# Decoder layer on one core: the low part of the mixing's gelu output is computed on GpSimd instead of VectorE

## The reference, cut to what matters

```
attn = (1 - LAMBDA_INIT) * rms(attn, g2)          # per head
attn = rms(attn, g3) + attn                        # "w" of a unit, 256 tokens x 256
h    = gelu(attn @ W1.T)                           # exact gelu
out  = h @ W2.T + attn
x    = x + out                                     # x1 of the unit
...
x = x + cross_attention(layernorm(x), ctx, ctx)    # second block
x = x + moe_ffn(layernorm(x))                      # third block, 8 experts with adapters
```

## Time and profile before

| | |
|---|---|
| median of 3 runs | 699.44 us (698.05 to 700.78) |
| profiled execution | 699.32 us, span of its rows 697.6 us |
| PE busy | 630.2 us, 90% |
| DVE busy | 505.7 us, 72% |
| ACT busy | 367.7 us, 53% |
| POOL busy | 265.1 us, 38% |
| chain that ended last | PE 76%, issue 7%, DVE 6%, DMA 3%, ACT 3%, POOL 2% |

### The profile page before, as it was taken

How to read it: one execution, slowest core, us unless ns; L and a number is a source line. 1 busy time by engine, 2 the same in 40 slices (tenths; PEclk the granted TensorE clock), 3 DMA queues, 4 the chain that set the end, 5 groups by cost and what they waited for, 6 DMA issues and landing times.

```text
span 697.6 us, 21651 instructions
## 1 busy us (share of the span) xinstructions
PE 630.2 (90%) x8338; PEld 591.6 (85%) x8338; DVE 505.7 (72%) x1242; ACT 367.7 (53%) x825; POOL 265.1 (38%) x361
## 2 busy tenths in 40 slices
PE   3789699799878787878999999999999999999997
PEld 3678577587667687767999999999999999999997
DVE  5586288687556988546887877788778877886672
ACT  3545457576673676533655455545554555455432
POOL 1212121221130554233455545554555455534322
PEclk9899999999988999996999999999999999999999
DMA  8684848567683476420001101110111011100000
GB/s 266 125 108 80 120 70 122 92 103 112 98 173 104 138 188 192 150 84 23 24 2 39 39 2 39 38 38 0 38 38 38 0 38 38 38 0 16 16 16 31
DMA packets 84140, 50.13 MB, mean 72 GB/s; under 512 B 31320, under 2 KB 83808, under 8 KB 84064
## 3 DMA queue, kind: packets, MB, share of 16 engines
q1 hardware_dynamic: 84064, 49.07, 31.9%
HBM read 23.88 MB, written 12.58 MB: 52 GB/s over the span
## 4 chain that ended last, share of the span: by engine, by line
PE 76%; issue 7%; DVE 6%; DMA 3%; ACT 3%; SPq 2%; POOL 2%; POOLq 0%; DVEq 0%; ACTq 0%
PE banks L698 58%; PE banks L824 5%; PE banks L753 3%; PE banks L842 3%; PE banks L860 2%; PE banks L983 2%; DMA m_w<-attn_scratch 2%; DMA attn_scratch<-h_wn 1%; POOL f_hT_lo L2138 1%; PE banks L767 1%; SPq L537 1%; DMA n_v<-in_L_attn_Wv_dram 1%; PE banks L722 1%; DVE wqkvT_lo L1542 1%; ACT h_t L1404 1%
## 5 line engine op out<-in xcount | busy, mean ns | idle before, releaser
L2138 POOL TENSOR_TENSOR f_hT_lo<-f_hs,f_hT_hi 128x512 fp32r<-128x512 f32 x64 | 87.3, 1365 | 102.8 <-ACT f_hT_hi L1377 99.2
L1841 DVE SCALAR_TENSOR_TENSOR f_hs<-banks,nbic,f_h 128x256 f32<-128x256 f32 x128 | 54.6, 479 | 40.6 <-PE banks L698 40.6
L698 PE MATMUL banks<-woT_hi,f_hT_lo 128*128 128x256 f32 x256 | 74.8, 292 | 0.2 <-POOL f_hT_lo L2138 0.2
L698 PE MATMUL banks<-f_adT_hi,lbT_lo 128*128 128x256 f32 x256 | 73.5, 287 | 0.0
L698 PE MATMUL banks<-f_xT_hi,wiT_hi 128*128 128x256 f32 x256 | 72.6, 284 | 0.0
L698 PE MATMUL banks<-f_xT_hi,wiT_lo 128*128 128x256 f32 x256 | 72.5, 283 | 0.0
L698 PE MATMUL banks<-woT_hi,f_hT_hi 128*128 128x256 f32 x256 | 72.4, 283 | 0.0
L698 PE MATMUL banks<-f_adT_lo,lbT_hi 128*128 128x256 f32 x256 | 72.4, 283 | 0.0
L698 PE MATMUL banks<-woT_lo,f_hT_hi 128*128 128x256 f32 x256 | 72.3, 283 | 0.0
L698 PE MATMUL banks<-f_xT_lo,wiT_hi 128*128 128x256 f32 x256 | 72.3, 282 | 0.0
L698 PE MATMUL banks<-f_adT_hi,lbT_hi 128*128 128x256 f32 x256 | 72.2, 282 | 0.0
(11 more groups left out here) (265 smaller groups left out, 2008.2 us busy)
## 6 DMA issues: line engine op xcount, KB each, us to landing
h_qk<-p_qk SPq DMA_DIRECT2D x64, 128.0 KB, 5.1
xin<-in_x_dram SPq DMA_DIRECT2D x16, 256.0 KB, 5.5
h_v<-p_v SPq DMA_DIRECT2D x128, 32.0 KB
attn_scratch<-h_wn SPq DMA_DIRECT2D x16, 256.0 KB, 4.6
m_w<-attn_scratch SPq DMA_DIRECT2D x16, 256.0 KB, 2.8
m_x<-in_x_dram SPq DMA_DIRECT2D x16, 256.0 KB, 3.4
x_scratch<-m_y SPq DMA_DIRECT2D x16, 256.0 KB, 2.2
c_x<-x_scratch SPq DMA_DIRECT2D x16, 256.0 KB, 2.8
```

The source lines that it names most:

```text
L698: ins = pe.matmul(acc, left(a), right(b), start=first and n == 0, stop=last and n == 2, skip_group_check=skip)
L1841: ins = dve.scalar_tensor_tensor(out=f_hs[:, j % 2, c * T:(c + 1) * T], in0=bank[HB[j]][:, c * T:(c + 1) * T], scalar=nbic[:, f:f + 1], in ...
L2138: pool.tensor_tensor(lo, f_hs[:, j % 2], hi.bitcast(F32), ALU.subtract).then_inc(f_hlo, 1)
```

## The change

The 16 splits leave DVE's order and are emitted on POOL. What is computed, its operands and its semaphores are the same. On POOL each split n stands behind the x-add of unit n+1 (behind the head step `head_rthird` too, for unit 5, and behind the last piece of `p_final` for unit 0); the splits 14 and 15 come after the last x-add. The orders of PE, ACT and SP are the same as before. The diff, cut in the middle of DVE's order:

```
@@ -1651,11 +1651,6 @@
             def m_low(u):
                 low(u, m_hi, flat(m_aT[u.slot][0][:, :, :]), flat(m_aT[u.slot][1][:, :, :]), bank[TURNED][:, :], m_lo)
 
-            def m_gsplit(u):
-                hi, lo = (flat(m_hT[u.slot][p][:, :, :]) for p in range(2))
-                dve.wait_ge(m_ghi, nth(u, 1, 1))
-                dve.tensor_tensor(lo, m_g[:, :], hi.bitcast(F32), ALU.subtract).then_inc(m_glo, 1)
-
             def m_residual(u):
                 dve.wait_ge(m_o, nth(u, 1, 1))
                 dve.wait_ge(m_xad, nth(u, 1, 1))
@@ -1946,17 +1941,14 @@
             go(4, head_normal, head_gain)
             go(0, m_low)
             go(1, m_low)
-            go(0, m_gsplit)
             go(6, head_masked(1, 0), head_masked(1, 1))
             go(2, m_low)
             go(4, head_added)
-            go(1, m_gsplit)
             go(7, head_masked(0, 0), head_masked(0, 1))
             clear_gate()
             go(0, m_residual)
             go(5, head_sums, head_newton)
             go(3, m_low)
-            go(2, m_gsplit)
             go(5, head_normal)
             go(1, m_residual)
             go(5, head_gain)
...
@@ -2018,11 +2000,10 @@
             go(14, m_low)
             go(12, m_residual)
             low_parts(LAST + 3, LAST + 4)
-            go(13, m_gsplit)
             go(15, m_low)
             go(13, m_residual)
-            go(14, m_gsplit, m_residual)
-            go(15, m_gsplit, m_residual)
+            go(14, m_residual)
+            go(15, m_residual)
 
 
 
@@ -2073,6 +2054,11 @@
                     pool.tensor_scalar(p_qk[:, u.slot, c], p_exp[:, c % 2], -1.0, headfac[:, 0:1] if c < KD else 1.0,
                                        ALU.add, ALU.mult).then_inc(p_fin, 1)
                 return emit
+
+            def m_gsplit(u):
+                hi, lo = (flat(m_hT[u.slot][p][:, :, :]) for p in range(2))
+                pool.wait_ge(m_ghi, nth(u, 1, 1))
+                pool.tensor_tensor(lo, m_g[:, :], hi.bitcast(F32), ALU.subtract).then_inc(m_glo, 1)
 
             def m_with_x(u):
                 if u.index == 0:
@@ -2162,29 +2148,45 @@
             go(0, m_with_x)
             go(1, m_with_x)
             go(7, p_final(3))
+            go(0, m_gsplit)
             go(4, head_rthird)
             go(2, m_with_x)
+            go(1, m_gsplit)
             go(3, m_with_x)
+            go(2, m_gsplit)
             go(0, c_rstds)
             go(5, head_rthird)
             go(0, c_constant)
             go(4, m_with_x)
+            go(3, m_gsplit)
             go(0, c_natural, c_with_bias)
             go(5, m_with_x)
+            go(4, m_gsplit)
             go(6, m_with_x, head_rthird)
+            go(5, m_gsplit)
             go(1, c_rstds)
             go(7, m_with_x)
+            go(6, m_gsplit)
             go(1, c_constant)
             go(8, m_with_x)
+            go(7, m_gsplit)
             go(1, c_with_bias)
             go(9, m_with_x)
+            go(8, m_gsplit)
             go(7, head_rthird)
             go(10, m_with_x)
+            go(9, m_gsplit)
             go(11, m_with_x)
+            go(10, m_gsplit)
             go(12, m_with_x)
+            go(11, m_gsplit)
             go(13, m_with_x)
+            go(12, m_gsplit)
             go(14, m_with_x)
+            go(13, m_gsplit)
             go(15, m_with_x)
+            go(14, m_gsplit)
+            go(15, m_gsplit)
 
 
 
```

More of the change, by code:

```diff
@@ L1652, in m_low @@
                 low(u, m_hi, flat(m_aT[u.slot][0][:, :, :]), flat(m_aT[u.slot][1][:, :, :]), bank[TURNED][:, :], m_lo)
[L1654 to L1657, removed]
             def m_residual(u):
@@ L1998, in _ @@
             go(1, c_clow)
-            go(9, m_gsplit)
             go(11, m_low)
```

12 lines of the change are left out of this document (removed).

## The result

The change made the kernel slower: 711.36 us median of 4 runs (707.60 to 713.77) against 699.02 us of the kernel before (698.05 to 700.78), ratio 1.0156 with a 95% interval of 1.0115 to 1.0196. Measured again beside the experiments, on another chip, it was 709.84 against 700.26 us, ratio 1.0135 (1.0093 to 1.0177). The forecast was 702.6 us, at most 707.0: the direction was the one that it leaned to, the size was three to four times too small. The profiled execution took 711.32 us, its span is 709.6 us.

The account below looks back on a forecast made before the run. The mixing was taken as bound by a chain of handovers, no engine being full, and the last stage by PE. Pass-by-pass terms summed to +3.2 us on 699.32, giving a 702.6 us median; range 699.6 to 707.0.

Parts of the forecast that it names:

- The cost of the operation: On POOL: a split takes 1.30 us, an x-add 1.28 once the split has left DVE.
- The new ready time: In the mixing: split ready 2.75 us after the residual add, 2.15 later than before.
- Pass 4 to 5, +2.1: Between residual adds 4 and 5: 6.45 us instead of 4.36, with the head step's root ahead of split 5 on POOL.
- in the range, not in the sum: Splits 6 to 8 meeting DVE's head steps: slowing of DVE and POOL counted only in the range 700.5 to 706.2 us.
- units 6 and 7, +0.6: Gelu 7 waits for split 6, and c_rr precedes x-add 8: +0.6 us, between 0 and one c_rr.
- pass 7 to 8, +0.8: Between residual adds 7 and 8: a pass as short as 4 to 5, lengthened by 0.8 us.
- I take only what the short passes need: Mixing, eleven passes: the average pass of 5.41 us exceeds the 5.2 minimum, so the 23.7 us upper bound is not charged.
- Up to unit 3 cost 0, relief -0.7: Units up to 3: splits ready long before PE needs them; DVE's relief brings m_aT_lo earlier, -0.7 us taken.
- The gelu of unit 11, +0.3: Passes 9 to 12: the gelu of unit 11 waits for split 10, +0.3 us.
- The last stage passes the shift on: From 312 us on PE is busy 377 of 386 us, so the mixing's 3.2 us shift passes on.
- 1 and 2: DVE's relief decides, 240 to 310 us: 694.1 us (chance 0.05); other slack swallows it: 699.5 to 700.4 us (chance 0.22).
- Rival 3: PE's clock and contention in the mixing: three more slow matmul groups, +3.9 us, 706.5 us; chance 0.15.

Follow-up runs that it names:

- the late splits ahead of the x-adds: Kernel before with splits 5 to 15 on POOL, each ahead of x-add n+1, splits 0 to 4 on DVE: 703.24 us, ratio 1.0033.
- early splits alone: Kernel before with only splits 0 to 4 on POOL, splits 5 to 15 still on DVE: 704.21 us, ratio 1.0055.
- a half: Changed kernel with POOL's split in two instructions of 128x256: 713.21 us, ratio 1.0170.
- the kernel before with the small gelu: Kernel before with one small gelu added on ACT at the place of c_psplit of unit 0: 698.48 us, ratio 0.9969.
- the small gelu: Changed kernel with one small gelu on ACT ahead of gelu 11's wait, run twice: 705.49 and 705.09 us, ratios 1.0068 and 1.0070.
- the kernel with extra matmuls: Changed kernel with 8 to 16 extra matmuls on PE ahead of the split wait, units 7 to 13: 711.08 us, ratio 1.0136.

## Why the prediction was wrong, step by step

Two steps failed: the contention of DVE and POOL was kept out of the sum, and the early units were taken as free. The table load was overlooked. What was right and what was not, term by term:

- **The cost of the operation** (1.30 us for a split, 1.28 for an x-add on POOL): right, 1.27 and 1.29 in the median.
- **The new ready time**: right. It put the split's end 2.75 us after the residual add's end, 3.43 after its start; the rows give 3.3 to 3.4 in seven of the units 5 to 14, and 4.6 with the root at unit 5 (forecast 1.27 more).
- **Pass 4 to 5, +2.1**: right, 6.41 against 4.36 us, +2.05. Pass 12 to 13, +0.7: 5.15 against 4.47. No pass from 4 to 13 was under 5.1 us.
- **Contention "in the range, not in the sum", and with it "units 6 and 7, +0.6" and "pass 7 to 8, +0.8"**: this step failed, for the part from unit 5 to 8. Together the passes from residual add 5 to 8 grew by 4.6 us in both profiles of the change, where the sum has 1.4. Split 7 was ready 5.2 us after residual add 6, not 3.4:

```profile
263.30 2.10 POOL L2070 TENSOR_TENSOR m_xa<-m_w,m_x 128x512 f32<-128x512 f32 x1 [0.20 <-DVE m_y L1659]
265.36 2.24 POOL L2061 TENSOR_TENSOR m_hT_lo<-m_g,m_hT_hi 128x512 fp32r<-128x512 f32 x1
...
264.78 1.70 DVE L1889 TENSOR_TENSOR h_wn<-h_wn,h_rh 128x1024 f32<-128x1024 f32 x1
```

  The x-add and the split each ran beside a large head step of DVE, and took 2.10 and 2.24 us, more than the bounds of 1.58 and 1.69 that made the range. The x-add of unit 9 took 2.09 us in the same way, so split 8 was ready at 4.2. `c_rr` cost nothing: it had ended before x-add 8 could start. A further 1.2 us of the 4.6 is one group of twelve at the lower clock, in pass 7 to 8 of the one profile and in pass 6 to 7 of the other.
- **"I take only what the short passes need"**: this held in part. Pass 6 to 7, with 5.27 us counted as long enough to hide a later split, paid 1.7 us, and 9 to 10 paid 1.0 to 1.1, which is the table load (below). The passes 10 to 11 and 11 to 12 grew by 1.3 and 2.6 us in the first profile, but by 0.1 and 0.3 in the second: that was the lower clock, from 294.57 to 302 us. 8 to 9 gave back 1.6 (forecast 1.0). The terms from unit 4 on came to +3.9; measured were +7.1 and +10.6 in the two profiles of the change, and only +1.2 with the late splits ahead of the x-adds.
- **"Up to unit 3 cost 0, relief -0.7"**: wrong in sign. The early part cost +2.1 and +3.1 in the two profiles, and early splits alone cost 4.4 us (0.27 to 0.84%). DVE lost one split of 1.03 us there (234.97 us before), but its small root steps now met POOL's full instructions, and `m_aT_lo` of unit 5 came 7.8 us after residual add 2 instead of 6.8. A view of before would have shown it: the same steps took 0.63 to 0.65 us in three rows beside POOL's pieces of 0.7 to 0.8 us (`c_ch_lo`, `c_x`), and 0.22 to 0.23 otherwise.

```profile
237.88 0.63 DVE L1888 TENSOR_TENSOR h_ss<-h_ss,h_rh 128x64 f32<-128x64 f32 x1
238.55 0.65 DVE L1889 SCALAR_TENSOR_TENSOR h_rh<-h_ss,h_rh 128x64 f32<-128x64 f32 x1
239.23 0.65 DVE L1886 SCALAR_TENSOR_TENSOR h_ss<-h_rh,h_ms 128x64 f32<-128x64 f32 x1
239.91 0.22 DVE L1888 TENSOR_TENSOR h_ss<-h_ss,h_rh 128x64 f32<-128x64 f32 x1
```

  The prediction priced contention by a large instruction (1.22 to 2.30 us), where it is worst for the smallest. The Trainium skill, "SBUF — State Buffer", Who interferes with whom, calls the shared port pair an exclusive lock, and says that a VectorE instruction with two SBUF inputs contends with a GpSimd instruction that reads SBUF. The trace agrees, and shows the price: it is the rest of POOL's instruction, 1.22 us beside a whole x-add and 0.65 beside a half. The other early cost is unit 4: its split stood behind x-add 5 (2.10 us) and was ready 4.2 and 5.2 us after residual add 3, so pass 3 to 4 grew by 0.3 and 1.3 us. A further 0.9 us of pass 2 to 3 is not the change's: PE's product of unit 3 ran at the lower clock (2.90 us against 1.95), and it did so (2.90 us) in the profile of the kernel before with the small gelu too.
- **The gelu of unit 11, +0.3**: mis-sized. The table load was overlooked: it stood ahead of the gelu and behind the new wait, 1.28 us in the row, and moving it shortened pass 9 to 10 by 1.3 us. The 0.5% that the small gelu gives in the measurements is more than this, and is not explained.
- **The last stage passes the shift on**: right. From residual add 15 to the end of the span it is 388.3 us before and 389.9 after.
- **Rivals.** 1 and 2 are refuted: DVE's relief gained nothing, and no slack swallowed the rest. Rival 3's number (706.5) was nearest. Its contention is shown; its clock gives one or two groups of 1.2 us on the path in the two profiles and is not the main cost, by the kernel with extra matmuls. The stated sign, a clock under 0.88 from 200 to 312 us, did not come (0.89). What lowers the clock is not told by the wait alone: the groups behind waits of 2.40 and 2.88 us ran slow in the change's profile, the one behind 2.92 us (267.65 us) took 1.69.

In sum, from the medians: 4.4 us for splits 0 to 4 and 8.2 for splits 5 to 15, and of the 8.2 some 4.8 for the place behind the x-add. The remaining 2 to 3.4 us I put to the longer operation with what it meets; no run shows this by itself. The table load behind the wait is 1.3 us of the 8.2 by the rows. What the small gelu gives beyond that stays open. The intervals are 2 to 3 us wide each way.

## What to carry to other kernels

Before moving an instruction to an engine with room in its sum, work out when it will be ready relative to the event that frees the instruction queued ahead of it, and charge that delay to every pass, unless a row shows what hides it, at the durations that the instructions have beside each other. Put the moved step ahead of the instruction that waits longest: here this alone was worth 4.8 us (1.4 to 8.3) with not one operation changed. If a dummy instruction makes a kernel faster, read in the rows whether what it should move has moved, and run it in the kernel before too. Then look at what runs beside it: the small VectorE steps near it on the path are those that pay, and so does a table load that sits behind the same wait.

## What the runs showed of the hardware

- A VectorE step of 0.23 us with two SBUF inputs lasts as long as the GpSimd instruction beside it: 1.19 to 1.23 us beside 1.27 to 1.29 us, 0.65 us beside halves of 0.70 us. The large ones stretch both ways: POOL's x-add and split of 128x512 took 2.10 and 2.24 us beside DVE's head steps of 128x1024, 1.29 and 1.27 us alone.
- The reload of gelu's table takes 1.28 us and waits with the gelu it precedes: it started at 287.23 us, when split 10 was done. The Trainium skill, "ScalarE: Activation LUTs", What ACT_TABLE_LOAD costs, gives about 1.28 us for the load and about 1.38 us for a drain, 2.66 together. The trace agrees with the first; a drain isn't seen in it, since the gelu starts 0.01 us behind the load (288.52 us).
- TensorE's granted clock differs between executions of one program. The twelve matmuls of unit 8's second product took 2.92 us in the first profile of the change and 1.69 in the second; those of unit 7's took 1.69 and 2.93. A pass of one profile against a pass of another is therefore safe only where such a group isn't in it.
